# Second loop of a two-layer graph network: a pair's one-hot matrix made on ScalarE in two halves instead of on VectorE in one piece

## The reference, cut to what matters

```python
h = jnp.maximum(_layernorm(x, axis=-1), 0.0)
...
em = jnp.concatenate([x[src], x[dst]], axis=-1)
em = jax.nn.relu(layer_norm(em @ msg_w + msg_b, msg_g, msg_beta))
em = em * edge_weights[:, None]
msgs = jax.ops.segment_sum(em, dst, num_segments=num_nodes)
...
messages = msgs / (counts + 1e-08) * valid
gate = jax.nn.sigmoid(x @ gate_w + gate_b)
combined = jnp.concatenate([x, messages], axis=-1)
h_new = jax.nn.relu(layer_norm(combined @ upd_w + upd_b, upd_g, upd_beta))
return gate * h_new + (1.0 - gate) * x
```

## Time and profile before

| | |
|---|---|
| median of 3 runs | 2285.07 us (2283.0 to 2289.69) |
| profiled execution, its own time | 2285.88 us |
| its span | 2283.7 us |
| busy over the span | DVE 78%, POOL 72%, PE 71%, ACT 45% |
| second loop of pairs | from about 1223 us to 2235 us of the span |

### The profile page before, as it was taken

The page is one execution under the profiler, slowest core; times in us unless marked ns, Lnnn a source line. Parts: engine busy times, 40 slices in busy tenths (PEclk is TensorE's granted clock), DMA queues, the critical chain, the costliest instruction groups (busy, mean ns, idle before and its releaser), DMA issues.

```text
span 2283.7 us, 44920 instructions
## 1 busy us (share of the span) xinstructions
PE 1618.7 (71%) x10025; PEld 1177.2 (52%) x10088; DVE 1772.2 (78%) x6299; ACT 1027.3 (45%) x3864; POOL 1646.1 (72%) x1744
## 2 busy tenths in 40 slices
PE   5488887777777777777775766667666666766766
PEld 4265555455555555555564545545455454554554
DVE  7777777676777676777768888887888878888786
ACT  5344444444444444444653444444444444445445
POOL 5777777777777777777147777777777777777774
PEclk9799999999999999999887888787888878888888
DMA  9433333323333323332242333332333333333222
GB/s 190 96 86 86 85 82 81 85 77 85 78 85 77 85 77 85 77 85 70 55 110 66 82 84 77 83 84 77 84 76 84 84 77 84 76 83 83 76 68 59
DMA packets 176818, 189.74 MB, mean 83 GB/s; under 512 B 100940, under 2 KB 132708, under 8 KB 176564
## 3 DMA queue, kind: packets, MB, share of 16 engines
q0 software_dynamic: 54192, 111.40, 19.3%
q1 hardware_dynamic: 120965, 75.89, 12.9%
q10 hardware_dynamic: 1472, 0.73, 0.2%
HBM read 172.91 MB, written 14.97 MB: 82 GB/s over the span
## 4 chain that ended last, share of the span: by engine, by line
PE 19%; DVE 15%; issue 14%; ACT 2%; DVEq 2%; ACTq 0%
PE psum L891 7%; PE psum L909 5%; PE psum L896 5%; DVE room L1811 3%; DVE room L1787 2%; DVE room L1797 2%; PE psum L718 1%; ACT room L1198 1%; DVEq L1525 1%; DVE rstd_e L1806 1%; DVE room L1886 1%; DVE dfar L1551 0%; DVE stats L1295 0%; ACT room L1186 0%; DVE room L1566 0%
## 5 line engine op out<-in xcount | busy, mean ns | idle before, releaser
L641 POOL DMA_INDIRECT room<-src_table,rec x1638 | 1570.1, 959 | 519.2 <-issue 477.7
L891 PE MATMUL psum<-room,ident 128*128 128x384 f32 (+1 forms) x512 | 292.4, 659 | 283.3 <-issue 200.3
L1186 ACT ACTIVATE room<-psum 128x128 f32<-128x128 f32 x832 | 219.3, 275 | 533.6 <-DVE room L1797 533.6
L818 PE MATMUL psum<-room 128*125 128x128 f32 x1664 | 254.5, 293 | 88.1 <-ACT room L1136 84.0
L909 PE MATMUL psum<-room 128*125 128x128 f32 x1664 | 273.8, 309 | 60.4 <-ACT room L1198 59.6
L1592 DVE TENSOR_TENSOR room<-psum,room 128x384 f32<-128x384 f32 (+1 forms) x256 | 151.0, 590 | 177.6 <-ACT room L1118 84.7
L818 PEld LDWEIGHTS psum<-room 128*125 128x125 f32 x1664 | 208.8, 193 | 139.6 <-ACT room L1136 138.8
L896 PEld LDWEIGHTS psum<-room 125*128 125x128 bf16 x2496 | 202.0, 114 | 149.3 <-issue 127.7
L909 PEld LDWEIGHTS psum<-room 128*125 128x125 f32 x1664 | 235.1, 214 | 69.6 <-issue 44.1
L1118 ACT ACTIVATE room<-psum 128x384 f32<-128x384 f32 (+1 forms) x256 | 130.4, 509 | 292.1 <-PE psum L790 288.6
L1811 DVE SCALAR_TENSOR_TENSOR room<-room,rstd_e,msg_beta 128x128 f32<-128x128 f32 x832 | 242.5, 349 | 10.2
(11 more groups left out here) (257 smaller groups left out, 2523.7 us busy)
## 6 DMA issues: line engine op xcount, KB each, us to landing
room<-dst_perm SPq DMA_DIRECT2D x128, 416.0 KB
room<-src_table,rec POOLq DMA_INDIRECT x1638
src_table<-rows SPq DMA_DIRECT2D x24, 224.0 KB
node_x<-in_x SPq DMA_DIRECT2D x5, 560.0 KB
x_rows<-node_x SPq DMA_DIRECT2D x12, 224.0 KB
out_rows<-node_x SPq DMA_DIRECT2D x12, 224.0 KB
rec<-rec_rows SPq DMA_DIRECT2D x125, 19.5 KB
pair_info<-pair_list SPq DMA_DIRECT2D x128, 2.0 KB
```

The lines of the kernel that those rows point to most:

```text
L641: pool.indirect_dma_start(out=xg[:, u, t * P:(t + 1) * P], out_offset=None, in_=table[:, :], in_offset=bass.IndirectOffsetOnAxis(ap=rec[:, ...
L818: i = nc.tensor.matmul(sum_bank[u % 2][0:W, 0:D], prob[:, c, t - t0, 0:W], xg[:, u, t * P:(t + 1) * P], start=(t == 0), stop=(t == T - 1), ...
L891: nc.tensor.matmul(msg_bank[b][:, cols], ident[:, :], xg[:, u, t0 * P:t1 * P], start=True, stop=False, skip_group_check=True)
L1186: i = nc.scalar.activation(sq[:, j * P:(j + 1) * P], msg_bank[b][:, j * P:(j + 1) * P], ACT.Square, accum_out=var_e[:, c, j:j + 1])
```

## The change

In the second loop VectorE no longer makes the one-hot. ScalarE makes it in two halves (tiles 0 to 7, 896 columns, and tiles 7 to 13, 768 columns), each by two passes: the square of node number minus destination, then one minus that, rectified (1 where they are equal, 0 elsewhere). The second pass waits for the first by a new semaphore `apart`. The first half stands in block 1 after `split_high`, the second in block 2 after `split_mid`; only the last pass counts up `oh`. For pair 0 both halves stand ahead of the loop. A constant column of ones is added. The first loop keeps its one-hot on VectorE.

```diff
+        one_col = sb("one_col", [P, 1])
...
+                self.apart = sem(f"apart{n}")
...
+            def one_hot(k, u, h):
+
+                s, v = msg, u % 2
+                cols = slice(BLK[2 * h][0] * P, BLK[2 * h + 1][1] * P)
+                act.wait_ge(s.id, k + 1)
+                ge(act, s.m, nth(k - 2, NB))
+                nc.scalar.activation(oht[0:W, v, cols], dstb[0:W, v, cols], ACT.Square, bias=node_id[0:W, v:v + 1],
+                                     scale=-1.0).then_inc(s.apart, 1)
+                act.wait_ge(s.apart, 2 * k + h + 1)
+                i = nc.scalar.activation(oht[0:W, v, cols], oht[0:W, v, cols], ACT.Relu, bias=one_col[0:W, :], scale=-1.0)
+                if h == 1:
+                    i.then_inc(s.oh, 1)
...
+                    if b in (1, 2) and there(k, -1, end):
+                        one_hot(k + 1, (u + 1) % U, b - 1)
...
             split_mid(msg, 0, 0)
+            for h in range(2):
+                one_hot(0, 0, h)
             all_pairs(act, msg_slot, last, 1)
...
                         if b == 1:
-                            one_hot(msg, k + 1, nxt)
                             msg_nodes(k + 1, nxt)
```

More of the change, by code:

```diff
@@ L1351, in _ @@
             dve.memset(eps_col[:, :], EPS)
+            dve.memset(one_col[:, :], 1.0)
             dve.memset(msg_b[:, 0:D], 0.0)
@@ L1561, in one_hot @@
                 ge(dve, s.m, nth(k - 2, NB))
[L1562 to L1566, removed]
+                dve.tensor_scalar(oht[0:W, v, :], dstb[0:W, v, :], node_id[0:W, v:v + 1], None, ALU.is_equal, ALU.add,
+                                  accum_out=cloc[0:W, u:u + 1]).then_inc(s.oh, 1)
             def mask(k, u, b):
@@ L1853, in _ @@
             split_rest(msg, 0, 0)
-            one_hot(msg, 0, 0)
             split_low(msg, 0, 0)
```

## The result

| | kernel before | changed kernel |
|---|---|---|
| median, same chip | 2286.85 us (2283.0 to 2289.69) | 2282.47 us (2278.42 to 2285.7) |
| ratio, 95% interval | | 0.9981 [0.9975, 0.9987] |
| span of the profiled execution | 2283.7 us | 2282.5 us |

The changed kernel is 4.4 us faster, inside the 0.3% that the prediction called no change, and 0.5 us from the predicted 2283. Counted as a change, though, 2.3 us was predicted and 4.4 measured; the medians of the kernel before, 2285.07 then and 2286.85 now, make up the rest of the closeness. The number was right. The way to it was not, as the rows show.

What follows compares the result with a forecast made beforehand. It took the second loop as bound by VectorE's chain to `split_low`, message and next scale, with GpSimd's gathers close behind. +5.0 for normal slots and -7.3 at jumps gave -2.3 us, so 2283 us, range 2277 to 2302.

Steps and rivals of the forecast that it cites:

- The passes: ScalarE, second loop: four new passes a slot, 1.03 us each for 896 columns and 0.92 for 768.
- The first matmul released by ScalarE's second pass: Second loop: ScalarE's one-hot, not VectorE's `split_low`, releases a pair's first matmul, 11.9 us after the slot's start.
- A normal slot: Second-loop slot without a jump: first matmul at 11.88 us against 11.78, +0.10 in 50 slots, +5.0 us.
- The prologue: Ahead of the second loop: four chained passes make the first message 3.1 us later, covered by VectorE's memset.
- no reciprocal waits for a root: Second-loop slot: ScalarE's root comes at 9.40 us, VectorE's reciprocal wants it at 9.84, so no stall.
- Rival A: Second half in normal slots: one-hot comes late, slower; 0.1 us more a pass gives 2303 us; chance 0.21 beyond 0.3%.
- rival C: ScalarE's loop jump takes over 5 us, squares start late, harmful from about 7 us; 0.02 with anything else.
- the term for the jump: 13 second-loop jumps: VectorE's chain decides, its 3.88 us jump loss stays, only 0.56 each saved, -7.3 us.
- nothing waits for it in this sum, it only moves the bound: GpSimd: without VectorE's one-hot the last gather comes up to 6 us earlier, counted as no gain in time.
- the 1.6 that it found to spare: End of the gathers: last ends 2227.87, its matmul starts 2229.47; other engines' speed-up cannot pass some 1.6 us.
- Matmuls that wait for gathers: Second loop, TensorE: listed as a sign that the forecast is wrong; no size given.
- rival B: Cheaper passes bring the one-hot in time; gathers then limit the gain to about 8 us, 2277 us; chance 0.13.

Runs made afterwards that it cites:

- b_w4: Kernel before, one-hot still on VectorE, less one implied wait in each slot of VectorE's second loop; 2284.41 us against 2285.84, ratio 0.9995.
- b_pad4: Kernel before, one-hot still on VectorE, with four tiny memsets ahead of the loops on VectorE; 2285.61 us, ratio 0.9995.
- a_same4: Changed kernel with four tiny memsets ahead and one more in each slot of VectorE's second loop; 2277.03 us against 2286.99, ratio 0.9959.
- a_len8: Changed kernel with two tiny memsets more in each slot of VectorE's second loop; 2279.72 us against 2285.84, ratio 0.9971.

## Why the prediction was right, and where it was not

**Right, with the sizes.** The passes: 1.03 and 0.92 predicted, 1026 and 919 ns for the first passes, 16 ns more for the second, which the prediction took as equal. The first matmul released by ScalarE's second pass (174.9 us of waiting named so). A normal slot: +0.10 predicted; over the 24 slots without a jump among the 32 above, the mean went from 15.17 to 15.27 us, and from slot start to first matmul from 11.87 to 11.92. The prologue: the first message at 1228.52 in place of 1222.99 (2.5 us of it are that execution's later start of the whole layer), covered by the memset as expected, and no reciprocal waits for a root. Rival A needed +0.15 a slot and does not come; nothing in the slots points to rival C. (With 0.1 us more a pass the prediction has 2303 in the rival and 2302 in the range: it is 2302.8.)

**Wrong: the term for the jump.** "*At a jump* VectorE's own chain decides ... VectorE through at 14.24 - 0.56 + 3.88 = 17.56 ... 13 x 0.56 = -7.3 us." I carried the 3.88 us over into the changed kernel as if it were a property of the jump. Measured over the eight jumps of the 32 slots, the jump slot went from 18.06 to 15.67 us, -2.4 each where -0.56 was predicted, some -31 us for 13. The page gave a means to doubt it: the queue of instruction packets, which I hadn't read. Taking an instruction out of a loop can take its fetch away: in `b_w4` one wait a slot did.

**Wrong: "nothing waits for it in this sum, it only moves the bound".** Had my jump term been right, that would have stood, but by the quicker gathers only: the 2.3 us of the sum are more than the 1.6 that it found to spare. With the jump slots short, the gathers are reached after the 44th pair. From the start of the 41st slot to that of the 64th the changed kernel takes 2219.63 - 1849.88 = 369.8 us where the kernel before took 2224.12 - 1864.76 = 359.4. "Matmuls that wait for gathers" was one of the prediction's own signs of being wrong, and it came. What stays is what the gathers allow. That is the mechanism of rival B (its reason was another: cheap passes), and its size: up to 6 us from quicker gathers and 1.6 to spare, so at most about 8; measured 4.4, and between the two profiled executions 3.9 is the gathers' pace. That the number was hit is luck, since the two wrong steps hide each other: -2.3 was summed from +5.0 and -7.3. From first to last slot the chip took 984.5 us in place of 991.2, -6.7 (2.3 of it given back by the later start of that execution's loop): +5 for the normal slots, -31 at the jumps, and so +19 of waiting for gathers.

**The gathers beside the one-hot.** Mean duration of one in the run of 767: 961 ns before, 961 in `b_w4`, 963 in `b_pad4`; 956 in the changed kernel, 954 in `a_same4` and in `a_len8`. Gathers over 1.0 us: 95, 91, 94 against 74, 56, 52. The trace of the kernel before shows where the difference lies: 93 of the 767 gathers overlap a one-hot in time and take 1014 ns on average, the other 674 take 954, about what gathers take where no one-hot is on VectorE (`b_w4` 1007 and 955, `b_pad4` 1033 and 953). 93 x 60 ns is 5.6 us. So the move itself is worth 4 to 6 us of gathers' pace, where 6 was the bound given; `b_w4` and `a_len8`, run on one chip, differ by 4.9 us in it, `b_pad4` and `a_same4`, on another, by 6.5. By the rule of the Trainium skill, page "SBUF — State Buffer", section "SBUF: two separate sides", GpSimd is blocked until the two-port operation ends. If the one-hot is such an operation, which no run shows, 0.65 us in each of 59 pairs make an estimate of up to 38 us. The trace shows about a sixth of it.

**Left open.** `a_same4` (2277.03 us, 0.9959) is the fastest of all: against its own runs of the kernel before its ratio, [0.9945, 0.9973], lies wholly below that of the changed kernel, [0.9975, 0.9987], though it does all the work of the changed kernel and some tiny memsets more. Its gathers take 964.36 us, `a_len8`'s 964.32, the changed kernel's 965.86. That makes 1.5 us. The profiled execution of `a_same4` spans 8.5 us less than that of the kernel before: 1.5 ahead of the gathers, 5.4 in them and 1.7 behind the last. The outer parts differ by as much between the other profiled executions, of both kinds of kernel (1256.9 to 1259.5 us ahead, 54.7 to 57.1 behind), so I can't name what `a_same4` has there, nor why 74 gathers are long in one and some 54 in the others. They weren't run on one chip with the changed kernel. No run has the one-hot on ScalarE and the fetch in place, so what the prediction assumed at the jump was never measured; `a_len8` was meant to be that run. Not tried either: loading a pair's record earlier, so that the gathers start earlier, and making VectorE's part of the first loop shorter, which stops 13 times for 2.8 to 3.5 us in both kernels.

## What to carry to other kernels

An "issue" wait at a loop's jump is not a fixed price: look at the instruction queue's packets, and if they come again in each pass, take a few instructions or waits out of that engine's loop and see whether they go (here, for one wait less a slot, a stop of 3.7 to 3.95 us became a wait of 1.4, and a slot with a jump fell from 18.06 to 15.68 us). Before counting on any saving, extend the second bound to the end of the stretch: two kernels that differ by 17 us over 32 slots ended 1.4 us apart. And a forecast that hits can do so with two large errors of opposite sign; here the slot by slot comparison showed them.

## What the runs showed of the hardware that was not expected

- A hardware loop on VectorE of 317 instructions (waits counted) at 1784 of its list is loaded again in each pass, 5 packets of 8192 bytes and 3.7 to 3.95 us of standing still (3.1 to 3.6 in `b_pad4`), and one of 313 at the same start isn't at all.
- On ScalarE a pass that reads 16-bit integers and writes bf16 costs what the plain passes of the earlier trace rows, with 0.09 us for the bias column, give for its width: 1026 ns for 896 columns, 919 for 768.
- A gather that GpSimd issues while VectorE makes a 1664-column one-hot takes 1014 ns on average, the others 954.
- The first loop's jumps cost VectorE 2.8 to 3.5 us from branch to next instruction, in both kernels.
- Two of the chips used take 3091 and 3094 us for the program that takes 2286 elsewhere, at a granted clock of 0.76 to 0.78 against 0.88 to 0.90; TensorE there pauses 2.6 us and the like between matmuls of one group, with no releaser shown. The cause wasn't looked for.
